# Silu and weighted one-hots on GpSimd, and a new order on VectorE and ScalarE, in the second half of a fused vision tower

## The reference

```python
# experts: two of eight for each token
routed_in = xf[flat_idx] * weights.reshape(-1, 1)
h_ = silu(grouped_mm(routed_in, w1, counts)) * grouped_mm(routed_in, w3, counts)
out = shared.at[flat_idx].add(grouped_mm(h_, w2, counts))

# polynomial attention: instead of a softmax, for each score x (0 where masked)
m = 1.0 / -100.0
lin = where((x >= -100) & (x <= 0), m * x + 1, 0)
poly = where(x > 0, x ** 2 + 1, 0)
att = (poly + lin) / 1000

# ternary feed-forward, on layernorm(h), with its own division by the rms
h = gelu(ternary_linear(x, w_up)); return ternary_linear(h, w_down)
def ternary_linear(x, w): return (x / (rms(x) + 1e-8)) @ ternary(w).T
```

## Time and profile before

| what | us |
|---|---|
| median of 3 runs | 842.32 (841.16 to 844.03) |
| the profiled execution, its own time | 843.61 |
| its span | 841.5 |
| TensorE busy in the span | 735.3 |
| VectorE busy | 647.9 |
| ScalarE busy | 409.8 |
| GpSimd busy | 77.9 |
| second half (slot 0 from about 452.9) | 388.6 |
| a slot in the loop | 47.6 |

### The profile page before, as it was taken

One profiled execution on the slowest core, in us unless ns is written; L12 is line 12 of the kernel. 1 busy time (PEld: TensorE's weight loads), 2 busy tenths in 40 slices (PEclk: granted clock), 3 DMA queues, 4 the chain that ended last, 5 costly groups with the idle time before them and its releaser, 6 DMA issues.

```text
span 841.5 us, 24887 instructions
## 1 busy us (share of the span) xinstructions
PE 735.3 (87%) x10567; PEld 514.5 (61%) x10567; DVE 647.9 (77%) x1447; ACT 409.8 (49%) x609; POOL 77.9 (9%) x68
## 2 busy tenths in 40 slices
PE   5879999999999999975795788999998999997857
PEld 3456666667676757654384556566765756565634
DVE  7667878888878888677586778988888998587653
ACT  4536454555546473542223282845547382644513
POOL 1101111110202020100000001000101001010000
PEclk9869999999999999975875999999999999999969
DMA  9024202020202000200000000000000000000000
GB/s 323 12 95 156 76 0 75 0 75 0 75 0 75 0 0 6 97 2 1 1 2 1 2 2 26 3 26 3 0 25 0 25 2 26 2 26 2 20 9 26
DMA packets 7371, 27.22 MB, mean 32 GB/s; under 512 B 2320, under 2 KB 3216, under 8 KB 5776
## 3 DMA queue, kind: packets, MB, share of 16 engines
q1 hardware_dynamic: 7312, 26.35, 8.4%
HBM read 22.15 MB, written 4.19 MB: 31 GB/s over the span
## 4 chain that ended last, share of the span: by engine, by line
PE 60%; DVE 22%; issue 9%; ACT 8%; DMA 0%; POOL 0%; DVEq 0%; POOLq 0%; SPq 0%; ACTq 0%
PE PS L372 10%; PE PS L321 6%; PE PS L741 6%; PE PS L383 5%; PE PS L476 4%; PE PS L706 4%; PE PS L362 4%; PE PS L465 3%; PE PS L418 3%; PE PS L433 3%; DVE mx L1290 3%; DVE Pm L1296 2%; ACT w_s L1015 2%; PE PS L451 2%; PE PS L683 2%
## 5 line engine op out<-in xcount | busy, mean ns | idle before, releaser
L890 ACT ACTIVATE PT<-PS 128x512 f32<-128x512 f32 x64 | 36.8, 596 | 78.4 <-PE PS L465 78.4
L362 PE MATMUL PS<-ident_s,xn 128*128 128x128 f32 x256 | 48.2, 304 | 25.5 <-DVE xn L1211 22.3
L719 PE MATMUL PS<-xT,wqkv_h 128*128 128x512 f16 x256 | 63.7, 394 | 6.0 <-ACT w_s L1015 4.5
L321 PE MATMUL PS<-tokW_h,w_s 128*128 128x256 f16 x504 | 58.5, 273 | 0.0
L883 ACT ACTIVATE Pm<-Pm 128x1024 f32<-128x1024 f32 x32 | 33.5, 1056 | 51.3 <-DVE Pm L1296 51.3
L362 PEld LDWEIGHTS PS<-ident_s,xn 128*128 128x128 f32 x256 | 31.0, 149 | 38.1 <-DVE xn L1211 21.0
L321 PEld LDWEIGHTS PS<-tokW_h,w_s 128*128 128x128 f16 x504 | 48.7, 98 | 5.8
L741 PE MATMUL PS<-tokW_h,work 128*128 128x256 f16 x448 | 51.4, 273 | 0.5 <-issue 0.5
L1290 DVE TENSOR_REDUCE mx<-PS 128x16 f32<-128x1024 f32 x32 | 39.0, 1220 | 16.3 <-PE PS L433 16.2
L372 PE MATMUL PS<-xT,wat_h 128*128 128x512 f16 x192 | 46.2, 400 | 4.5 <-DVE xT L1592 4.5
L719 PEld LDWEIGHTS PS<-xT,wqkv_h 128*128 128x128 f16 x256 | 22.7, 100 | 44.0 <-ACT w_s L1015 17.9
(11 more groups left out here) (245 smaller groups left out, 1636.8 us busy)
## 6 DMA issues: line engine op xcount, KB each, us to landing
work<-in_x SPq DMA_DIRECT2D x7, 1536.0 KB, 6.9
out<-H SPq DMA_DIRECT2D x8, 512.0 KB, 2.6
w_s<-in_w SPq DMA_DIRECT2D x3, 1024.0 KB, 7.0
work<-in_x SPq DMA_DIRECT2D x3, 512.0 KB, 5.9
wup_s<-in_wup SPq DMA_DIRECT2D x1, 1024.0 KB, 4.8
wdn_s<-in_wdn SPq DMA_DIRECT2D x1, 1024.0 KB, 8.3
w_s<-in_tokW SPq DMA_DIRECT2D x3, 256.0 KB, 4.1
wup_s<-in_wqkv SPq DMA_DIRECT2D x1, 768.0 KB, 7.5
```

The costliest lines, as they stand in the source:

```text
L321: m = pe.matmul(dst, halves_[xi][:, k, rows], w[:, wi, k, cols], start=(n == 0), stop=(n == 3 * chunks - 1))
L362: m = pe.transpose(PS[:, bank, t * P:(t + 1) * P], xn[:, t, c * P:(c + 1) * P], ident_s[:, :])
L719: m = pe.matmul(PS[:, UP_BANKS[f % 3], :], wup_h[:, c, f * P:(f + 1) * P], part[:, c, :], start=(k == 0), stop=(k == 2 * C - 1))
```

## The change

The silu moves from VectorE to GpSimd, as two passes a half, tz*wz into tz and wz+tz into wz, each waiting for the one before. The weighted one-hots move to GpSimd too, and from slot g+1 to the end of slot g. `stats3` runs one slot ahead: `stats3(1)` before slot 0, `stats3(g+2)` in slot g behind `v_x4T`, with GpSimd's power between the two halves of the silu. `norm3` now opens VectorE's slot, and `one_hots` stands ahead of `projected`. All eight `g_parts` (low halves) come ahead of both polys of tiles 0 and 1. The linear part of tile 0 moves from ScalarE to VectorE, and ScalarE takes the linear parts of tiles 2 and 3 ahead of their squares. In `norm4` both powers are 0.5, and r4 = 1/(sqrt(v) + 1e-8 * sqrt(v+eps)) takes two small operations instead of four.

```diff
@@ TensorE @@
-                pe.wait_ge(lin_ok, 3 * g + 3)        # routed_sums, and before the x3 transposes
+                pe.wait_ge(lin_ok, 2 * g + 2)
@@ B2_scores, t == 2 @@
-                    pe.wait_ge(lin_ok, 3 * g + 1)
-                    pe.wait_ge(linv_ok, g + 1)
+                    pe.wait_ge(linv_ok, 2 * g + 2)
@@ ScalarE, a_B3 and slot_B @@
                         relus(g + 1, 1)
-                        lins(g + 1, 0)
...
                     relus(g, t)
+                    lins(g, t)
                     quads(g, t)
-                    lins(g, t)
@@ GpSimd @@
+            def silu(g, k):
+                cols = slice(k * RB * HID // 2, (k + 1) * RB * HID // 2)
+                pool.wait_ge(tz_ok, 2 * g - 1 + k)
+                pool.tensor_tensor(tz[:, cols], tz[:, cols], wz[:, cols], ALU.mult).then_inc(silu_step, 1)
+                pool.wait_ge(silu_step, 4 * g - 3 + 2 * k)
+                pool.tensor_tensor(wz[:, cols], wz[:, cols], tz[:, cols], ALU.add).then_inc(silu_step, 1)
+            def weighted_hots(g):
+                pool.wait_ge(silu_step, 4 * g - 4)
+                pool.wait_ge(oh_ok, g - 1)
+                pool.tensor_tensor(one_hot_w, one_hot, wt[:, bass.ds(RB * (g - 2), RB)].unsqueeze(2)
+                                   .broadcast_to([P, RB, 64]), ALU.mult).then_inc(weighted_ok, 1)
             def slot_B(g, prev, nxt, routed=None):
-                if nxt:
-                    p_rstd(ve3_ok, g + 2, ve, rstd, rstd3_ok)
                 if prev:
                     p_rg(g - 1)
                 p_ln4(g, 0)
                 p_ln4(g, 1)
+                if routed in ("first", "batch"):
+                    silu(g, 0)
+                if nxt and not (isinstance(g, int) and g == LAST - 1):
+                    p_rstd(ve3_ok, g + 3, ve, rstd, rstd3_ok)
+                if routed in ("first", "batch"):
+                    silu(g, 1)
+                    weighted_hots(g + 1)
+            p_rstd(ve3_ok, 2, ve, rstd, rstd3_ok)
@@ VectorE: silus and weighted_hots are gone; v_lin @@
-                dve.wait_ge(lin_ok, 3 * g + 1)
-                dve.tensor_scalar(lin[1][:, :].rearrange("p (i n) -> p i n", i=4), PS[:, 0:4, 256:512], 0.0, -0.01,
-                                  ALU.min, ALU.mult).then_inc(linv_ok, 1)
+                for t in range(2):
+                    hb = t * 256
+                    if not first(g):
+                        dve.wait_ge(f2_ok, TILES * g + t - 1)
+                    dve.wait_ge(relu_ok, TILES * g + 2)
+                    dve.tensor_scalar(lin[t][:, :].rearrange("p (i n) -> p i n", i=4), PS[:, 0:4, hb:hb + 256],
+                                      0.0, -0.01, ALU.min, ALU.mult).then_inc(linv_ok, 1)
@@ norm4 @@
-                dve.tensor_tensor(rr[:, ts], rq[:, 1, ts], rq[:, 0, ts], ALU.mult).then_inc(r4_step, 1)
+                dve.scalar_tensor_tensor(out=rr[:, ts], in0=rq[:, 0, ts], scalar=1e-8, in1=rq[:, 1, ts], op0=ALU.mult,
+                                         op1=ALU.add).then_inc(r4_step, 1)
...
+                dve.reciprocal(r4[:, ts], rr[:, ts]).then_inc(r4_step, 1)
@@ VectorE, slot_B @@
                 if nxt:
-                    stats3(g + 1)
+                    norm3(g + 1)
                 if prev:
                     mean_squares(g - 1)
                 turned(g, 0, 4)
-                if nxt:
-                    norm3(g + 1)
-                if routed in ("batch", "last"):
-                    weighted_hots(g)
-                projected(g, 0, 5)
                 if routed == "batch":
                     dve.wait_ge(weighted_ok, g - 1)
                 if routed in ("first", "batch"):
                     one_hots(g - 1)
+                projected(g, 0, 5)
...
                 v_x4T(g)
-                if routed in ("first", "batch"):
-                    silus(g)
+                if nxt and not (isinstance(g, int) and g == LAST - 1):
+                    stats3(g + 2)
                 if nxt:
                     v_quads(g + 1, 0)
                     v_quads(g + 1, 1)
                     v_lin(g + 1)
-                g_parts(g, 0, 4)
+                g_parts(g, 0, NF)
                 if nxt:
                     poly(g + 1, 0)
-                g_parts(g, 4, NF)
-                if nxt:
                     poly(g + 1, 1)
```

More of the change, by code:

```diff
@@ L775, in slot_B @@
                 if nxt:
-                    pe.wait_ge(lin_ok, 3 * g + 3)
+                    pe.wait_ge(lin_ok, 2 * g + 2)
                     for c in range(C):
@@ L1070, in _ @@
             relus(0, 1)
-            lins(0, 0)
             routed_tables()
@@ L1147, in _ @@
                 dve.memset(buf[:], v).then_inc(setup_v, 1)
-            for k, v in ((0, -0.5), (1, 0.5)):
+            for k, v in ((0, 0.5), (1, 0.5)):
                 dve.memset(pq[:, k, :], v).then_inc(setup_v, 1)
@@ L1549, in gates_in @@
                     dve.tensor_tensor(half_batch(k), z, weighted(k, g), ALU.mult).then_inc(wz_ok, 1)
-            def silus(g):
-                for k in range(2):
-                    cols = slice(k * RB * HID // 2, (k + 1) * RB * HID // 2)
-                    dve.wait_ge(tz_ok, 2 * g - 1 + k)
-                    dve.scalar_tensor_tensor(out=wz[:, cols], in0=tz[:, cols], scalar=1.0, in1=wz[:, cols],
-                                             op0=ALU.add, op1=ALU.mult).then_inc(silu_step, 1)
-            def weighted_hots(g):
-                dve.wait_ge(silu_step, 2 * g - 2)
-                dve.tensor_tensor(one_hot_w, one_hot, wt[:, bass.ds(RB * (g - 2), RB)].unsqueeze(2)
-                                  .broadcast_to([P, RB, 64]), ALU.mult).then_inc(weighted_ok, 1)
             def gated_sums():
@@ L1595, in poly @@
             def poly(g, t):
-                if t == 1:
-                    dve.wait_ge(linv_ok, g + 1)
+                if t < 2:
+                    dve.wait_ge(linv_ok, 2 * g + t + 1)
                 else:
-                    dve.wait_ge(lin_ok, 3 * g + max(t, 1))
+                    dve.wait_ge(lin_ok, 2 * g + t - 1)
                 if t < 2:
@@ L1619, in v_lin @@
             def v_lin(g):
-                if not first(g):
-                    dve.wait_ge(f2_ok, TILES * g)
-                dve.wait_ge(lin_ok, 3 * g + 1)
-                dve.tensor_scalar(lin[1][:, :].rearrange("p (i n) -> p i n", i=4), PS[:, 0:4, 256:512], 0.0, -0.01,
-                                  ALU.min, ALU.mult).then_inc(linv_ok, 1)
+                for t in range(2):
[5 more added lines that the diff above has]
+                                      0.0, -0.01, ALU.min, ALU.mult).then_inc(linv_ok, 1)
             def turned(g, pair, bank):
@@ L1652, in norm4 @@
                 dve.wait_ge(rstd4_ok, 2 * g + pair + 1)
-                n = 8 * g + 4 * pair
-                dve.tensor_tensor(rr[:, ts], rq[:, 1, ts], rq[:, 0, ts], ALU.mult).then_inc(r4_step, 1)
+                n = 4 * g + 2 * pair
+                dve.scalar_tensor_tensor(out=rr[:, ts], in0=rq[:, 0, ts], scalar=1e-8, in1=rq[:, 1, ts], op0=ALU.mult,
+                                         op1=ALU.add).then_inc(r4_step, 1)
                 dve.wait_ge(r4_step, n + 1)
-                dve.tensor_scalar(rr[:, ts], rr[:, ts], 1e-8, None, ALU.add).then_inc(r4_step, 1)
+                dve.reciprocal(r4[:, ts], rr[:, ts]).then_inc(r4_step, 1)
                 dve.wait_ge(r4_step, n + 2)
-                dve.reciprocal(rr[:, ts], rr[:, ts]).then_inc(r4_step, 1)
-                dve.wait_ge(r4_step, n + 3)
-                dve.tensor_tensor(r4[:, ts], rr[:, ts], rq[:, 0, ts], ALU.mult).then_inc(r4_step, 1)
-                dve.wait_ge(r4_step, n + 4)
                 normalize(g, xn2, mv2, r4, xn4_ok, tiles)
@@ L1792, in _ @@
             row_codes()
+            stats3(1)
             slot_B(0, False, True)
```

## The result

The changed kernel takes **849.77 us** (847.46 to 849.92, five runs) against 842.32 of the kernel before (840.72 to 844.29, five runs beside it): a ratio of 1.0081, 95% interval 1.0059 to 1.0104. It is slower by 7.45 us; forecast were +3.5, a time of 845.8 and a range of 830.5 to 852. The profiled execution has a span of 848.0 us (841.5 before).

What follows compares the result with a forecast made beforehand. TensorE was taken as the bound, busy 44.79 of 47.6 us in a looped slot. Four routed boundaries at +2.55 (+10.2) less 6.7 elsewhere gave +3.5 us, a median of 845.8 us, range 830.5 to 852.

Steps and rivals of the forecast that it cites:

- The collision term: Boundaries after slots 1 to 4: GpSimd and VectorE passes exclude each other, x3 transposes 2.55 us later each, +10.2 us.
- Rival 1: Routed boundaries: VectorE never waits, only GpSimd does; they gain 1.1 us each, 831.2 us in all; chance 0.33.
- rival 2: Routed boundaries: collisions delay the low halves by 2.8 us, not 3.65, so the change breaks even, about 842 us; chance 0.07.
- rival 3: GpSimd's pass truly takes 3.3 us, 859.6 us in all; chance 0.05 together with a low clock.
- The fixed part: Everything outside the four routed boundaries, norm4's edit in eight slots included: -6.7 us.
- the unrouted boundaries: Boundaries 0/1 and 5/6, without silus: x3 transposes start earlier as ScalarE's chain ends earlier, -1.1 us each.
- The wait for cnt: Expert choice: the additional linear pass lies bare on VectorE's serial chain, TensorE waits +1.1 us.
- From the count to the first x3 transposes: Start of slot 0: linear before square on ScalarE lets the transposes start 1.0 us earlier.
- At 6/7: Boundary without x3 transposes: the whole gain of -1.4 us reaches the values.
- The norm4 edit: Two small operations fewer per pair on VectorE: 0.4 us in each of eight slots, -3.2 us.
- The clock: Forecast TensorE gaps of 2.6 us might lower its clock, some microseconds a slot; chance 0.05 together with rival 3.

Runs made afterwards that it cites:

- e5: Changed kernel with silu and weighted one-hots back on VectorE, in the middle of the next slot: 835.02 us, ratio 0.9909 to the kernel before.
- e6: Changed kernel with the silu's first half left on GpSimd, second half and one-hots on VectorE in the middle of the next slot: 836.37 us, ratio 0.9918.
- e13: Changed kernel with products of a constant that nobody reads put into TensorE's waits in slots 6 and 7: 842.26 us, ratio 1.0012.
- e9: Kernel before with the new norm4 alone: 839.06 us, ratio 0.9977.
- e8: Changed kernel with fifteen 128x128 fp32 products more on TensorE's serial chain of the expert choice, as a delay: 849.97 us, ratio 1.0097.
- e7: Kernel before with fifteen 128x128 fp32 products more on TensorE's serial chain of the expert choice, as a delay: 849.52 us, ratio 1.0083.
- e12: e5 with 85 products of a constant that nobody reads put into TensorE's waits in slots 6 and 7: 830.04 us, ratio 0.9878.
- e14: e12 with such fillers also ahead of the x3 transposes in every slot, and 12 in slot 0: 831.41 us, ratio 0.9902.
- e15: e12 with 50 fillers instead of 85 in slots 6 and 7: 826.66 us, ratio 0.9823.
- e3: Changed kernel with each of GpSimd's five passes over a quarter of its columns, output not the reference's: 837.42 us, ratio 0.9945.

## Why the prediction was right, and where it was wrong

The sign, the range and the mechanism of the collisions were right; the sum came out 4 us low, and two of its terms were off in opposite directions.

*The collision term was right.* +2.55 us for a routed boundary was forecast; measured are +2.63 in the loop (25.11 against 22.48), +2.03 at the first routed one and +2.4 at the last. Step by step, counted from the scores of tile 0: low halves over after 17.7 forecast (644.15 less 626.43), 17.7 measured (694.08 less 676.42); poly of tile 0 over after 20.1, measured 20.05; the transposes after 25.0, measured 25.1. But the inside differs, and the agreement is partly luck. A pass takes 2.35 us, not 2.1. Against that only the second square was held, not both. The first half of the silu ended 4.2 us after the scores (680.60), not 3.3, and the power for the next statistics (680.70) followed it, so the first square (680.85) began ahead of the second product (681.69). And the one-hots did hold the low halves (5.39 against 3.69), which the prediction had laid beside the linear parts. The linear parts ended 11.2 us after the scores, not 12.9; the low halves paid the difference.

The Trainium skill (SBUF — State Buffer, Who interferes with whom) states an exclusive lock, which the engine that issues first holds for its whole instruction while the other waits. The trace agrees on both sides: 3.12 instead of 1.22 us on VectorE, 3.22 instead of 2.36 on GpSimd. The estimate of 2.25 us a pass, from the Trainium skill (GPSIMD Engine Reference, Performance versus the Vector engine), was nearer than my 2.1: measured are 2.35. (By the prediction's own layout it would have cost a boundary 0.35 us more, not 0.45, since the one-hots there lie beside the linear parts.) Rival 1, VectorE never waits, falls with the same rows; so does rival 2, since e5 puts the collisions at 3.58 us a boundary and not 2.8, and rival 3, since a pass takes 2.35 us. The looped slot of 46.1 us of rival 1 is near what e5 and e6 show without collisions at that place, 46.05 and 45.6; e5's has 0.5 us more behind the transposes than the changed kernel's (24.53 against 24.05).

*The fixed part was right at the boundaries and too small behind them.* Forecast -1.1 at the unrouted boundaries: 23.89 became 22.77, and 22.47 became 21.34 at 5/6. The wait for cnt grew from 5.28 to 6.31, where +1.1 was forecast. From the count to the first x3 transposes it is 8.30 us and not 9.46, where -1.0 was forecast. At 6/7 scores 0 to scores 2 of slot 7 would give -0.9 and not -1.4 (10.23 in e13, whose clock is at 1.00 there, against 11.14). The norm4 edit was -0.4 a slot in e9. What I missed: the eight x3 transposes now take 1.09 us and not 1.73. Before, they were drawn out by rows that came one by one; now all rows lie ready. From the transposes to the next scores a looped slot gained 1.03 us (25.08 to 24.05) where 0.4 was forecast. That makes the looped slot 49.15 us and not 49.7, and is worth some 0.6 us in each of seven slots, about -4.

*The clock was the term that failed.* I gave it no cost in the sum, a part of the upper end, and 0.05 of chance together with another rival, from the argument that gaps of 1.14 us leave the clock at 1.00 and that only the forecast gaps of 2.6 us could lower it. The long gaps never came (1.9 us was the longest in a looped slot), and the clock fell all the same, at five places of the second half where it had not before. The largest makes the scores of tile 0 to those of tile 2 of slot 7 last 14.88 us; they took 11.14 before, and the same order takes 10.23 in e13, where the clock stays up, so it cost 4.65. Two of the short ones cost 1.7 us each where TensorE is busy (behind the boundaries 2/3 and 4/5: 25.73 against 24.05, and 27.95 against the 26.26 of e8, which has no fall there). The other two lie ahead of a wait, as the down-products with 5.33 instead of 3.67, and the wait takes them up. That is some 8 us. From slot 1 to the end, the changed kernel's profiled execution lost 7.1 us. Its boundaries give +7.4 (six of them, -1.1, +2.0, +2.6, +2.6, +2.4, -1.1). The stretches behind them give -6.3 and the last slot -2.0 without these falls. The sum is about -1 us, and 8 are the clock's. The fillers bear out its sign: with them the changed kernel is at 842.3 us, equal to before (ratio 0.9987 to 1.0037). This is not like for like, for they also shortened the rest of slot 7 from 60.1 to 57.7 us, and the kernel before was never given any.

So by this reckoning the change would be worth next to nothing without the falls: four collisions of 3.6 us take what eight slots gain. The forecast of +3.5 had the right sign and half the size of the measured +7.45, and it is luck that it came so near: a missed gain of about 4 stood against a missed loss of about 8.

*Open.* Why one thin stretch brings a fall and an equal one does not is not settled: e7 and e8 show that the same instructions may have a fall or not, but not whether the time at which they come decides it; in the traces of e12, e13, e14 and e15 it is gone where TensorE's waits were filled. Why fillers in the other slots bring nothing in the median (e14) is open too; four runs between 824.1 and 835.2 us don't tell. Nor was it tried to give GpSimd all its passes at times when VectorE only reads PSUM, or to put fillers into the kernel before.

## What to carry to other kernels

Moving a pass with two SBUF inputs from VectorE to an idle GpSimd takes it off no shared resource: price it by GpSimd's duration (2.35 us for what VectorE does in 1.22, and here two passes for one), and look at what VectorE runs beside it; here the passes beside PSUM reads and waits were free (e6), and those beside the squares and low halves were not. Where TensorE is near its bound, the same work can take 5 us more or less through the clock (359.3 and 364.0 us, 366.4 and 360.7 here), so compare kernels by stretches with the same granted clock before a reason is given for a small difference. Filling TensorE's waits with products that nobody reads is worth a try in a thin stretch, if they are cut to end before the wait does.

## What was not expected of the hardware

- A one-input VectorE operation of 128x4 in SBUF was held by a GpSimd pass (1.32 us instead of 0.17, at 679.31 in the changed kernel), while statistics passes (1.39 us at 677.59) and passes that read PSUM (1.21) went on beside GpSimd at their usual length. Held time stands inside an instruction's duration, not in the idle time before it.
- GpSimd's pass of 128x1024 with two full fp32 inputs takes 2.35 us alone; the mask product of the earlier trace rows, with a bf16 output, 1.90; the one-hots, with an fp16 input, last 2.21 to 2.33, but always beside low halves of VectorE. As they hold one of these for 1.7 us (2.39 instead of 0.68), some 0.5 us of their duration would be a wait of their own; that is an estimate from the two figures. A silu pass over a quarter of the columns took 0.72 (e3).
- The same instructions from slot 1 to the end took 359.3 and 364.0 us, and 366.4 and 360.7, in single executions that differ in what ran ahead of slot 1.
